# The start stage of a recurrent block kernel in two halves, and its first turns of the loop written out

## What is computed

```
xn = layernorm(x)                        # over the 128 columns, 1e-5
out = x + mamba(xn) * silu(stack(xn))

q, k, v = split(shift(x) @ Wqkv)         # stack, per layer; shift: half the columns one token later, per head 64 wide
q, k = l2norm(q) * qs, l2norm(k) * ksc   # then rotary tables cos, sin, scale
sim = q . k * 8, masked to the window and the one before; attn = softmax(sim)
x = x + (attn @ v) @ Wo
x = x + (a * gelu(gate)) @ W2,  [a, gate] = layernorm(shift(x)) @ W1

h = x * rsqrt(mean(x*x) + 1e-6) * rms_w  # mamba block, x is xn
x1, g = split(h @ in_W + in_b); x1 = silu(causal conv4(x1))
delta, B, C from x1;  hc = exp(delta*A) * hc + delta*B*x1;  y = hc . C
out = (silu(g) * y) @ out_W + residual
```

## Time and profile before

| | us |
|---|---|
| median of three runs | 1774.46 |
| lowest, highest | 1773.91, 1774.90 |
| the profiled execution | 1775.65 |
| its span | 1773.90 |
| PE busy | 1691.0 |
| VectorE busy | 1530.2 |
| Pool busy | 1405.5 |
| ScalarE busy | 1252.3 |

### The profile page before, as it was taken

How to read it: one execution, slowest core, us unless ns; L and a number is a source line. 1 busy time by engine, 2 the same in 40 slices (tenths; PEclk the granted TensorE clock), 3 DMA queues, 4 the chain that set the end, 5 groups by cost and what they waited for, 6 DMA issues and landing times.

```text
span 1773.9 us, 73872 instructions
## 1 busy us (share of the span) xinstructions
PE 1691.0 (95%) x30944; PEld 983.5 (55%) x30944; DVE 1530.2 (86%) x2724; ACT 1252.3 (71%) x2325; POOL 1405.5 (79%) x1264
## 2 busy tenths in 40 slices
PE   3889999999999999999999999999999999999986
PEld 1455555555555555555555555555555555555552
DVE  5768998889889889889998898888998989988976
ACT  3566687766876767867778668677687677776764
POOL 1667878977889788888879887897788888788872
PEclk9899999999999999999999999999999999999998
DMA  3013233141312422133321323314131242212340
GB/s 113 22 40 66 56 75 86 39 100 41 78 44 53 105 62 60 29 72 81 82 65 34 71 51 85 83 39 93 42 90 32 53 108 65 54 32 56 75 94 24
DMA packets 94054, 113.13 MB, mean 64 GB/s; under 512 B 42318, under 2 KB 59484, under 8 KB 93724
## 3 DMA queue, kind: packets, MB, share of 16 engines
q1 hardware_dynamic: 93724, 108.41, 25.9%
HBM read 19.22 MB, written 1.05 MB: 11 GB/s over the span
## 4 chain that ended last, share of the span: by engine, by line
PE 66%; DVE 16%; issue 7%; POOL 6%; ACT 3%; POOLq 0%; DVEq 0%; ACTq 0%
PE bank L630 13%; PE bank L655 9%; PE bank L714 9%; PE bank L646 7%; PE bank L731 6%; PE bank L675 5%; PE bank L692 4%; DVE qn L1321 3%; PE bank L759 3%; DVE qc L1321 3%; DVE ssq L1328 2%; PE bank L774 2%; POOL hb L1644 2%; PE bank L667 2%; POOL AB L1599 2%
## 5 line engine op out<-in xcount | busy, mean ns | idle before, releaser
L1599 POOL TENSOR_TENSOR AB<-qc,qn 128x512 f32<-128x512 f32 x384 | 487.0, 1273 | 107.3 <-DVE qn L1321 105.9
L1610 POOL TENSOR_TENSOR AB<-AB,rinv 128x512 f32<-128x512 f32 x384 | 391.3, 1043 | 35.0 <-DVE rinv L1344 35.0
L630 PE MATMUL bank<-wqkv,XT 128*128 128x512 f32 x768 | 383.8, 602 | 3.8 <-DVE qn L1321 3.7
L1617 POOL TENSOR_TENSOR Pb<-Pb,p_rden 128x512 f32<-128x512 f32 x192 | 200.3, 1043 | 149.3 <-DVE p_rden L1365 147.6
L1004 ACT ACTIVATE qkT<-bank 128x512 f32<-128x512 f32 x384 | 228.8, 596 | 107.8 <-PE bank L655 106.3
L995 ACT ACTIVATE sq<-bank 128x512 f32<-128x512 f32 x384 | 228.4, 595 | 96.6 <-PE bank L630 96.5
L1328 DVE TENSOR_REDUCE ssq<-sq 128x8 f32<-128x512 f32 x384 | 258.5, 673 | 8.3 <-ACT sq L995 7.5
L1321 DVE TENSOR_TENSOR qc<-bank,rt 128x512 f32<-128x512 f32 x384 | 258.7, 674 | 7.5 <-ACT sq L995 5.5
L1321 DVE TENSOR_TENSOR qn<-bank,rt 128x512 f32<-128x512 f32 x384 | 261.5, 681 | 0.0
L714 PEld LDWEIGHTS bank<-PT,V 64*64 64x64 f32 x12288 | 197.0, 134 | 95.3 <-issue 89.2
L655 PE MATMUL bank<-ident,AB 128*128 128x128 f32 x1536 | 243.5, 281 | 4.5 <-ACT qkT L1004 3.3
(11 more groups left out here) (145 smaller groups left out, 2498.4 us busy)
## 6 DMA issues: line engine op xcount, KB each, us to landing
V<-V SPq DMA_DIRECT2D x672, 64.0 KB
rep<-du SPq DMA_DIRECT2D x64, 512.0 KB, 4.7
wqkv<-in_Wqkv SPq DMA_DIRECT2D x36, 256.0 KB, 3.6
XV<-XT SPq DMA_DIRECT2D x96, 64.0 KB, 2.1
wo<-in_Wo SPq DMA_DIRECT2D x6, 512.0 KB, 5.3
BC<-BC SPq DMA_DIRECT2D x8, 256.0 KB
w<-in_W SPq DMA_DIRECT2D x6, 341.0 KB, 5.0
BC<-BC SPq DMA_DIRECT2D x8, 128.0 KB
```

The costliest lines, as they stand in the source:

```text
L630: pe.matmul(R[u % 2][:], XT[:, s % NB, (u % 2) * P:(u % 2 + 1) * P], wqkv[:, (u // 2) * 512:(u // 2 + 1) * 512], start=True, stop=True).th ...
L1599: pool.tensor_tensor(AB[:, n % NAB, :], qc[:, u % 2, :], qn[:, u % 2, :], ALU.add).then_inc(rs_done, 1)
L1610: pool.tensor_tensor(o, o, r, ALU.mult).then_inc(nm_done, 1)
```

## The change

The start stage loads `x` in four pieces (each with its semaphore) and the identity behind the first; constants and scales come ahead of the small weights. It works in two halves of eight tiles: `stats` and `gather`, an estimate for each half, and `norm_rows`, which does (x - mean) * rstd in one operation for each 128x128 tile. `mean_square` gets the mean square from rstd squared times the variance, so squaring and summing over 2048 columns go. Transposes use four banks. The state `ST` is no more copied by ScalarE but by two transfers from `XT` behind the barrier (`take_state`), awaited in `res_attention(0)`. Of the four `HT` copies two are VectorE's. The memsets, `identb`, `maskb` and the first `rt` are made ahead of the barrier. The turns -2, -1 and 0 are replaced by lists written out for each engine; in step 0 the guard, the estimate and `norm_q` are done in two halves (tiles 0 to 3 and 4 to 7), and `z_x(0)`, `z_tap(0)`, `z_conv(0)` and `z_silu(0)` stand among the work of step 0. From turn 1 on the lists are as before.

```diff
-STEADY = range(-2, LAST)
+FIRST = 1
+STEADY = range(FIRST, LAST)
...
+            for n in range(PIECES):
+                sp.dma_start(xin[:, n * NP:(n + 1) * NP, :], x[:, n * NP:(n + 1) * NP, :]).then_inc(x_in[n], 16)
+                if n == 0:
+                    sp.dma_start(k.ident[:], t["c_ident"]).then_inc(ident_in, 16)
             for dst, src in k.consts:
                 sp.dma_start(dst, src).then_inc(k.const_in, 16)
             load_qks(sp, t, k, 0)
+            for dst, src in loads:
+                sp.dma_start(dst, src).then_inc(small_in, 16)
...
+            for q in range(4):
+                z, h = q // 2, q % 2
+                half = slice(h * NH2, (h + 1) * NH2)
+                act.wait_ge(var_done, q + 1)
+                act.activation(lnv[:, z, half], var[:, z, half], ACT.Ln).then_inc(guess_done, 1)
+                act.wait_ge(guess_done, 2 * q + 1)
+                act.activation(guess[:, z, half], lnv[:, z, half], ACT.Exp, scale=-0.5).then_inc(guess_done, 1)
...
-                    act.activation(k.ST[:, pair, :], src, ACT.Copy).then_inc(tp_copied, 1)
...
+            def norm_rows(h):
+                for i in range(h * NH2, (h + 1) * NH2):
+                    ins = dve.tensor_scalar(XN[:, i, :], xin[:, i, :], st2[:, i, 0:1], rstd[:, 0, i:i + 1], ALU.subtract, ALU.mult)
+                ins.then_inc(xn_norm, 1)
+
+            def mean_square(h):
+                r, q = rstd[:, 0, half(h)], msq[:, half(h)]
+                link(dve.tensor_tensor(q, r, r, ALU.mult))
+                link(dve.tensor_tensor(q, q, st2[:, half(h), 1], ALU.mult))
+                dve.tensor_scalar(var[:, 1, half(h)], q, 1e-6, None, ALU.add).then_inc(var_done, 1)
...
-            link(dve.tensor_tensor(XN[:], xin[:], row(msq[:]), ALU.subtract))
...
-            link(dve.tensor_tensor(HN[:], XN[:], XN[:], ALU.mult))
-            link(dve.reduce_sum(msq[:], HN[:], AX_X))
...
+            def take_state():
+                for h in range(2):
+                    q = slice(h * DH, (h + 1) * DH)
+                    sp.dma_start(ST[q, :, :], XT[q, :, h:h + SEQ]).then_inc(st_in, 16)
+
+            arrange_x(0)
+            take_state()
+            for n in range(4):
+                spread(0, n)
...
-            pe.wait_ge(const_in, k.CONST_IN)
-            pe.wait_ge(pool_set, POOL_SET)
-            pe.wait_ge(mask_set, 2)
+            qk(0, 0)
+            qk(0, 1)
+            z_x(0)
+            qk(0, 2)
+            qk(0, 3)
+            qk(0, 4)
+            qk(0, 5)
+            qk(0, 6)
+            turn(0, 0)
+            qk(0, 7)
+            turn(0, 1)
+            value(0, 0)
+            scores(0, 0)
...
+            square(0, 7)
+            copy_qk(0, 1)
+            copy_v(0, 0)
+            guess_q(0, 1)
+            copy_v(0, 1)
+            copy_qk(0, 2)
+            expo(0, 0)
...
+            square(1, 0)
+            expo(0, 1)
+            square(1, 1)
...
+            square(1, 4)
+            z_silu(0)
+            copy_p(0, 1)
+            expo(0, 2)
...
+            sum_squares(0, 7)
+            guard_q(0, 1)
+            softmax(0, 0)
+            norm_q(0, 1)
+            sum_p(0, 0)
+            z_conv(0)
+            rotate(1, 0)
...
-            pool.wait_ge(k.const_in, k.CONST_IN)
-            for tl in range(TILES):
-                tables(0, tl)
+            rotate_sum(0, 4)
+            normalise(0, 0)
+            normalise(0, 1)
+            rotate_sum(0, 5)
...
```

## The result

The changed kernel took 1760.03 us (median of 4 runs, 1757.64 to 1760.83) and the kernel before, on the same chip, 1774.68. The ratio is 0.9913 with a 95% interval of 0.9902 to 0.9925: 14.65 us less, 0.87%. The forecast was 1756.9 with a range of 1752.5 to 1762. The profiled execution took 1760.83 (span 1758.8) against 1775.65 (1773.90): 15.1 less in the span.

What follows compares the result with a forecast made beforehand. TensorE (95% busy) and VectorE (86%) fill all but the first 44 us slice. The four parts put rinv of pass 1 at 75.2, lead 17.6: 1775.65 - 17.6 = 1758.05, less 1.2 for the median: 1756.9, range 1752.5 to 1762.

Steps and rivals of the forecast that it cites:

- Part 1: Start stage to its last instruction: end moves from 33.84 to 22.6, 11.2 us off.
- rival 2: Start bound elsewhere: landing at 9.5, or row operations 0.3 beside Pool's tables; lead 14.5, 1760 us; chance 0.15.
- the term of row operations: Start stage: eight 128x128 row operations per half at 0.20 each, 1.6 a half, between 1.0 and 2.6.
- Part 2: Barrier to first rotation: 2.95 us instead of 8.3, first rotation at 25.55, lead 16.6.
- Part 3: First rotation to first softmax: before 26.4 us, now first softmax at 45.15, lead 23.4.
- Rival 1: Clock stays full in pass 0: first softmax about 43.5, waits 2.5, lead 19.8, 1754.7 us; chance 0.2.
- rival 3: Halves don't bring the scores forward: first softmax near 49, lead 13.8, 1760.7 us; chance 0.1.
- Part 4: First softmax to rinv of pass 1: 27.0 work plus 2.9 waits, rounded to 30.05, ending at 75.2, lead 17.6.
- rival 5: Clock stays at half in pass 1 after the wait for Pool's six tiles: 1779 us and above; chance 0.04.
- The hand-over: From rinv of pass 1 to pass 1's first softmax: 7.6 us, softmax near 83.
- The lead is kept: From the entry of pass 1 to the end: the 17.6 us lead carries through, rows 17 to 18 earlier.
- rival 4: Lead given back before pass 1: state copy holds the spreads 14 us or more, 1771 to 1778; chance 0.05.

Runs made afterwards that it cites:

- number 2: The changed kernel with step 0's guard, estimate and norm_q in one piece for 64 columns, first tiles' turns behind tile 7; 1767.94 us, ratio 0.9965.
- number 8: The changed kernel with memsets, the two casts (on VectorE) and the rotation tables behind the barrier again; 1762.07 us, ratio 0.9931.
- number 5: The changed kernel with the squaring pass and its sum put back for each half; 1763.93 us, ratio 0.9939.
- the two repeats: The changed kernel itself, unedited, run again on two more chips; 1759.51 us (ratio 0.9911) and 1761.00 us (ratio 0.9923).
- number 3: The changed kernel with square(1,1) and copy_p(0,0) ahead of expo(0,1) on ScalarE; 1757.94 us, ratio 0.9909.
- the first of 7: The changed kernel with square(1,1), copy_p(0,0), z_silu(0) ahead of expo(0,1), and values_out(0,0) ahead of qk(1,3); first run 1757.61 us, second 1756.28.
- Number 4: The changed kernel with two unread dummy products on PE ahead of turn(0,4), where it stood idle; 1756.71 us, ratio 0.9893.
- number 1: The changed kernel's start stage and constants with the old turns and one estimate for 64 columns; 1763.65 us, ratio 0.9942.

## Why the prediction was right, and where it missed

**Part 1, start stage.** Forecast 11.2 off, measured 10.2. The first XT copy came 1.2 late (16.54, not 15.3). The landing was no obstacle in this profile (against rival 2's first half, and the estimate from the bandwidth rule): the pieces were worked on from 3.57 and 5.17 on, and none after was waited for. In other profiles the second piece was taken up as late as 5.96 (the changed kernel) and 6.59 (number 2), so the landing does cost there, up to 1.4 us over this profile, and rival 2's first half was right in kind. The miss is the term of row operations: 0.267 each (2.14 for eight), not 0.20, which is 16 x 0.067 = 1.1. Pool worked only from 8.65 to 10.34 and so beside neither half: rival 2's second half came true in half its size, but not by its reason. Small operations beside Pool's tables (0.37, 0.31 and 0.38 for three that take 0.17 elsewhere, and in number 8 at this very place) cost 0.5 more, and 0.4 was regained behind. The page "VectorE: DVE Perf Modes" of the Trainium skill (perf-mode tier table) gives float32 tensor_scalar in SBUF the 2x rate, in a table for 2048 columns. This trace shows no gain from it at this width: 128 columns of tensor_scalar with two per-partition scalars took longer (0.267) than the statistics of as many (0.205). By number 5 a us here is about a us at the end (4.2 at the stage's end, 3.5 to 4.2 behind it).

**Part 2.** 2.95 forecast, 2.24 measured: two projections took 2.81 instead of 3.7. In the two repeats they took 3.75, as priced, and 1.95 or 1.96 in number 3 and the first of 7. So the durations show both speeds from one start to the next, and this part's 0.7 was the chance of one execution. The granted-clock column doesn't tell it: it reads 1.00 over 24 to 28 in the repeats, as it did at 36 to 38 before.

**Part 3.** 19.6 forecast, 18.24 measured. Rival 1 was right for the larger part, with a granted clock of 1.00 over 30 to 38 and single projections of 1.10 there; then it was 0.50 over 40 to 42, inside the stretch that the forecast had named. The gap at tile 2 was 0.65, not 1.2. Against that stands a cost that I hadn't seen: two operations of 32 columns, priced near 0.2, took 0.75 and 1.26. The rows above show why: the first ends with Pool's tensor_tensor (33.95 + 0.75 = 34.70; 33.40 + 1.26 = 34.66), the second starts 0.05 after Pool's next and ends 0.05 after it (37.28, 37.23); the same rinv without Pool beside it took 0.19 at 45.70. In both the operation ends only when Pool's is over. The page "SBUF — State Buffer" of the Trainium skill (SBUF: two separate sides) has the port pair that VectorE and GpSimd share as an exclusive lock, which whoever starts first holds for the whole instruction while the other is fully blocked. The trace agrees (0.75 and 1.26, ending within 0.05 of Pool's), and the earlier trace rows had the hint, a cast of 1.05 beside Pool's memsets. The two took 0.55 + 1.07 = 1.6 more than priced. The second is on the path: Pool's first scaling starts at 37.36, 0.08 behind this rinv, and PE's first turn at 38.46 had waited 1.32 for it. The halves were right in direction and, by number 2, worth 8.4 within these lists; rival 3 is out (44.16, not 49).

**Part 4 was mis-sized.** 30.05 forecast, 32.64 measured, and the difference of 2.6 is in the waits: 5.56 instead of 2.9. Three of them came as forecast (0.77 for 0.9, 1.18 for 1.25, 0.90 for 0.7). The fourth, 2.71, is the step that I left out: I had priced what `expo(0, 1)` costs the square behind it, but not the copy of P behind it, on which PE hangs, nor what PE's idle time then does to the clock. I had asked for the clock in rival 1 (full) and rival 5 (half in pass 1), never within pass 0's second half, though the earlier trace rows showed 0.50 behind a wait at 62 to 64. Number 4 shows the cause by itself, and the four profiles with a shorter half clock put the size of this term at 1.25 to 1.47 in one execution and 2.71 to 2.73 in another.

**The hand-over** took 7.53 for 7.6: right in number, and by luck: both this kernel and the one before had a share of half clock in it (before, 7.61 with a granted clock of 0.80 over 92.82 to 100.43), and each of the nine profiles with full clock there had 5.93 or 5.94. The forecast took the 7.6 from the rows without asking for the clock in it. Rival 5 had named this place; the half clock came there, but was over by 80.

**The lead is kept.** Lead at pass 1 forecast 17.6, measured 16.0; at the end 15.1. Over the 12 profiles of the table the end differs from pass 1 by +1.2 to -3.6, with a mean of -1.3. So the step is right to about 1 us, and wrong by up to 4 in a single execution. The places are few. Between the rinv of pass 1 and that of pass 2, the nine profiles with full clock at the hand-over gain 1.6 on that of before. From one later rinv to the next no lead fell by more than 1 us except at nine places, each with a granted clock of 0.95 or 0.96 over the pass where before reads 1.00: between passes 2 and 3 in six profiles (1.7 each), 16 and 17 in number 1 (2.1), 27 and 28 in the first of 7 (2.6) and in 8 (2.8). The losses behind pass 47 are told above. The misses in the lead are -1.1 (stage), +0.7 (barrier), +1.4 (part 3) and -2.6 (part 4), so 1.6 at pass 1, and 0.9 after: 15.1 instead of 17.6. Two of the misses, 2.1 together, went the other way, and one of them was the chance of the first clock; without them the lead would have been 13.0. The repeats had 14.0 and 12.6 at the end, so the forecast's 17.6 was too high in all three.

**The transfers** cost nothing, as forecast; rival 4 is out.

**Open:** what sets the speed of the first projections, how long half clock lasts behind the same idle stretch, and whether it comes at the hand-over and in the last pass. Dummy products in the last pass weren't tried.

## What to carry to other kernels

Go through a written-out list and ask at each instruction that waits what stands behind it with its inputs ready, and who hangs on that, PE first: here one exp ahead of a square and a copy cost 3.9 us of VectorE's time (1.18 + 2.71), or 2.4 where half clock was shorter. The new order of three lines gave it back in pass 0 (4.0), and with the silu step the whole run was 3.1 less (1.4 to 4.9). Where PE is thinly used, an idle stretch has two prices, itself and the half clock behind it; cheap dummy products tell the two apart in one run. Where leads of 1 to 3 us are compared, take the profile at fixed places (a rinv per pass) and not the end, and look at the granted clock between them: one half-clocked stretch cost 1.7 to 2.8 in a pass here, as much as such a lead.

## What the runs showed of the hardware

- **The clock behind a short idle.** PE idle for 2.42 (busy 0.81 of 3.20) was followed by 0.50 over six us; busy 2.77 of 3.20, by 1.00. The matmuls in those six us were 72 and 150. Half clock followed that idle in all seven profiles that have it, and was about twice as long in three of them as in the other four.
- **One kernel's runs differ by 3 to 8 us on one chip** (1757.36 to 1765.32 on the widest, for the changed kernel), and it goes with the clock: of its 15 executions the four below 1758 us had a mean granted clock of 0.994 to 0.996, the three above 1762 us 0.989 to 0.991.
- **VectorE and Pool.** A VectorE operation of 0.2 can take 1.26 beside a Pool tensor_tensor of 1.26, and two of 0.17 took 0.31 and 0.38 beside Pool's tables. Larger ones (rotations from PSUM, 0.67 to 0.69) show nothing of it.
- **Row operations.** A float32 tensor_scalar of 128 columns with two per-partition scalars took 0.267, the statistics of 128 columns 0.205 (1.64 for eight).
